# Gates that begin with x's rows, a feed-forward entered inside the attention, and scatters dealt over more rounds

## The reference

```python
x = x + L0_xattn(layernorm(x), ctx, ctx, gates)    # gates: tanh(cat(q,k,v) @ W + b), log_sigmoid, cumsum, running max
x = x + L0_ffn(layernorm(x), w1, b1, w2, b2)       # rmsnorm, rows rounded to 255 levels, weights to -1/0/1, gelu, the same again
x = x + L1_xattn(layernorm(x), ctx, ctx)           # phi = (elu + 1)**5, causal scores, normalised
x = x + L1_ffn(layernorm(x), gate, 8 experts)      # softmax over 8 experts, the best 2, gelu feed-forward of each
```

## Time and profile before

| | us |
|---|---|
| median of 3 runs | 611.01 (609.58 to 611.13) |
| the profiled execution: its time, its span | 610.62, 608.9 |
| busy: PE, DVE, ACT, POOL | 497.8, 399.3, 303.2, 352.3 |
| gates, first attention, feed-forward | 0 to 46.4, to 137.3, to 250.9 |
| second attention with routing, experts | to 365.7, to 608.9 |

### The profile page before, as it was taken

One profiled execution on the slowest core, in us unless ns is written; L12 is line 12 of the kernel. 1 busy time (PEld: TensorE's weight loads), 2 busy tenths in 40 slices (PEclk: granted clock), 3 DMA queues, 4 the chain that ended last, 5 costly groups with the idle time before them and its releaser, 6 DMA issues. The chain is left out here.

```text
span 608.9 us, 13847 instructions
## 1 busy us (share of the span) xinstructions
PE 497.8 (82%) x4467; PEld 365.9 (60%) x4467; DVE 399.3 (66%) x1228; ACT 303.2 (50%) x752; POOL 352.3 (58%) x421
## 2 busy tenths in 40 slices
PE   1979999997688878367666658999999999999960
PEld 1845776663355444246556526788878887888740
DVE  3432678998888888456988635566657676666540
ACT  0234575863789988567764313444344434443410
POOL 3509599782888878524686661445555555455531
PEclk9979999997999999857776678999999999999995
DMA  8733633320132232110142264233223323332225
GB/s 280 120 96 121 209 104 114 105 71 18 36 105 92 83 102 73 38 35 23 56 156 87 79 175 133 42 49 54 48 43 54 53 49 53 45 55 30 26 28 154
DMA packets 50614, 50.14 MB, mean 82 GB/s; under 512 B 21584, under 2 KB 40272, under 8 KB 50384
## 3 DMA queue, kind: packets, MB, share of 16 engines
q1 hardware_dynamic: 41168, 36.04, 20.2%
q0 software_dynamic: 7152, 9.36, 9.7%
q10 hardware_dynamic: 2224, 3.86, 2.0%
HBM read 36.46 MB, written 14.87 MB: 84 GB/s over the span
## 5 line engine op out<-in xcount | busy, mean ns | idle before, releaser
L1394 ACT ACTIVATE region<-cps,aux 128x128 f32<-128x128 f32 x312 | 89.3, 368 | 132.3 <-PE cps L1546 132.3
L1285 POOL CAST vaug<-region 128x512 bf16<-128x512 f32 x78 | 49.1, 630 | 107.9 <-ACT region L1394 96.2
L1546 PE MATMUL cps<-aux,w1hi 128*128 128x128 bf16 x1248 | 109.9, 219 | 0.9 <-DVE aux L1754 0.5
L1546 PE MATMUL cps<-aux,w1lo 128*128 128x128 bf16 x624 | 107.5, 217 | 0.0
L1559 PE MATMUL cps<-w2pair,vaug 128*128 x312 | 105.3, 379 | 0.0
L1546 PEld LDWEIGHTS cps<-aux,w1hi 128*128 x1248 | 95.9, 96 | 5.8 <-DVE aux L1754 0.7
L1562 PE MATMUL cps<-w2pair,vaug 128*128 x312 | 78.7, 273 | 0.0
L1291 POOL DMA_INDIRECT y_sum<-aux x39 | 61.0, 1564 | 15.7 <-issue 6.0
L1546 PEld LDWEIGHTS cps<-aux,w1lo 128*128 x624 | 61.5, 98 | 0.0
L1761 DVE TENSOR_TENSOR vaug<-region,vaug 128x512 bf16<-128x512 f32 x78 | 51.2, 697 | 0.1
L1769 DVE TENSOR_TENSOR aux<-cps,wstage 128x256 f32<-128x256 f32 x39 | 16.6, 425 | 52.7 <-PE cps L1559 51.7
(11 more groups left out here) (274 smaller groups left out, 1113.2 us busy)
## 6 DMA issues: line engine op xcount, KB each, us to landing
wstage<-in_wall SPq DMA_DIRECT2D x64, 256.0 KB, 2.6
aux<-row_buf SPq DMA_DIRECT2D x39, 129.5 KB, 2.1
x_all<-in_x SPq DMA_DIRECT2D x4, 512.0 KB, 8.9
w2pair<-in_ctxT ACTq DMA_DIRECT2D x2, 1024.0 KB, 11.5
vaug<-in_ctx SPq DMA_DIRECT2D x16, 128.0 KB, 4.0
aux<-in_ctxT SPq DMA_DIRECT2D x8, 256.0 KB, 3.0
y_sum<-x_all SPq DMA_DIRECT2D x8, 256.0 KB, 3.2
w2pair<-in_w1T SPq DMA_DIRECT2D x2, 512.0 KB, 4.7
```

The source lines that it names most:

```text
L1285: pool.tensor_copy(hhi[:, j % 3, n], hf[:, j % 2, n]).then_inc(hi_done, 1)
L1394: last = act.activation(hf[:, j % 2, f * BLK:(f + 1) * BLK], hp[:, j % 2, f, :], ACT.Gelu, bias=b1T[:, bass.ds(e * NF + f, 1)])
L1546: last = pe.matmul(hp[:, j % 2, f, :], w1(cc * NF + f, part), rowsT[:, j % 2, cc, xpart, :], start=(cc == 0 and n == 0), stop=(cc == NC - ...
```

## The change

1. Gates: TensorE transposes the first quarter of x's rows before the context's matmuls, which come in two halves, behind the first and the second quarter. VectorE takes the statistics of the first quarter before the gates' weights. The eight unused matmuls at the block's end go, and four open the attention's block.
2. Feed-forward: ScalarE centres tiles 0 and 1 within the attention's last rounds; VectorE scales tile 0 right behind the last `product`; the first rounding comes before the roots of sequence 6; the first table covers 8 tiles, not 4 (so the next `row_scales` and `tables` come later). `refined`, `scaled` and `residual` of the last sequence move into the tile loop, and so do the `row_stats` of sequence 5; those of 6 and 7 come two or three tiles later. 8 unused matmuls follow the first transposes in place of 16 ahead of them.
3. Routing: the scatters are dealt over the rounds by a table. Rounds 6 and 7 issue six in place of four each, and after the last `low_part` eight are left in place of twelve.
4. Ahead of the experts: 44 unused matmuls before the wait for the last scatters (28 before), and 5 behind it (10 before).

```diff
@@ gates, TensorE
-                    pe.wait_ge(zb_ready, 1)
-                    for half in range(2):
+                    def context_gates(half):
+                        if half == 0:
+                            pe.wait_ge(zb_ready, 1)
                         pe.wait_ge(kt_in[half], 16)
...
                         last.then_inc(tp_ready, 1)
+                        if q < 2:
+                            context_gates(q)
                         if q:
                             gates(q - 1)
...
-                    keep_running(8)
@@ gates, VectorE (gate_weights: the six operations that stood first)
-                        if q:
+                        if q == 0:
+                            gate_weights()
+                        else:
                             normalize(q - 1)
@@ attention and feed-forward, TensorE
+                    for _ in range(4):
+                        pe.matmul(unread, identb[:, :], flat(heads[:, 0:HG, :]), start=True, stop=True)
                     state(0)
...
-                    pe.wait_ge(pv1_read, B)
-                    keep_running(16)
                     first_transposes(0)
+                    pe.wait_ge(pv1_read, B)
+                    keep_running(8)
@@ ScalarE
-            SCALED_AT = (0, 4, 12, NT)
+            SCALED_AT = (0, 8, 12, NT)
...
+                        if n >= UN - 3 and n < UN - 1:
+                            centred(n - UN + 3)
-                    centred(0)
-                    centred(1)
-                    centred(2)
+                    first_rounded(0)
                     roots(B - 2)
                     squares(B - 1)
-                    first_rounded(0)
                     first_rounded(1)
+                    centred(2)
@@ GpSimd
-                    residual(B - 1)
...
-                        if i < 2:
-                            row_scales(i + 1)
+                        if i in (3, 5):
+                            row_scales((i - 1) // 2)
...
+                        if i == 0:
+                            residual(B - 1)
@@ VectorE
+                        if n == UN - 1:
+                            first_scale(0)
                     joined(B - 1)
-                    refined(B - 2)
-                    scaled(B - 2)
-                    denominators(B - 1)
-                    square_sums(B - 1)
-                    first_scale(0)
-                    row_stats(B - 3)
                     first_scale(1)
                     first_copied(0)
+                    denominators(B - 1)
+                    refined(B - 2)
+                    square_sums(B - 1)
                     first_copied(1)
-                    refined(B - 1)
-                    scaled(B - 1)
+                    scaled(B - 2)
...
-                        if j < 2:
-                            row_stats(B - 2 + j)
                         if j + 2 < NT:
                             first_scale(j + 2)
+                        if j == 1:
+                            refined(B - 1)
+                            scaled(B - 1)
+                        if 2 <= j <= 4:
+                            row_stats(B - 5 + j)
@@ routing, GpSimd
+            SCATTERED = {4: ((0,), (1,)), 5: ((2,), (3,)), 6: ((4,), (5, 6)), 7: ((7,), (8, 9)), 8: ((10,), (11,)), 9: ((12, 13), ())}
...
-                    for b in range(ENDS - 4, B):
-                        scatter(b, 0)
-                        scatter(b, 1)
+                    for i in range(NT - TB, NT):
+                        scatter(i)
@@ ahead of the experts, TensorE
-                    keep_running(28)
+                    keep_running(44)
                     pe.wait_ge(moved[(B - 1) % NPK], 16 * 2 * TB * (B // NPK))
-                    keep_running(10)
+                    keep_running(5)
```

More of the change, by code:

```diff
@@ L387, in _, with gate_weights @@
                     chain = Chain(dve, ch)
-                    dve.wait_ge(small_in, 48)
-                    dve.wait_ge(made, 1)
-                    for gate_, at in ((0, 56), (1, 120)):
-                        n = slice(gate_ * NH, gate_ * NH + NH)
-                        dve.tensor_copy(Z[:, 0:NC, at:at + NH], wif[:, 0:NC, n])
-                        dve.tensor_tensor(Z[:, NC:2 * NC, at:at + NH], wif[:, NC:2 * NC, n], wif[:, 2 * NC:3 * NC, n], ALU.add)
-                    dve.tensor_scalar(ifb, ifb, 1.0 / CAP, None, ALU.mult)
-                    dve.tensor_scalar(gain, gain, 1.0, None, ALU.add).then_inc(zb_ready, 1)
+                    def gate_weights():
+                        dve.wait_ge(small_in, 48)
+                        dve.wait_ge(made, 1)
+                        for gate_, at in ((0, 56), (1, 120)):
+                            n = slice(gate_ * NH, gate_ * NH + NH)
+                            dve.tensor_copy(Z[:, 0:NC, at:at + NH], wif[:, 0:NC, n])
+                            dve.tensor_tensor(Z[:, NC:2 * NC, at:at + NH], wif[:, NC:2 * NC, n], wif[:, 2 * NC:3 * NC, n], ALU.add)
+                        dve.tensor_scalar(ifb, ifb, 1.0 / CAP, None, ALU.mult)
+                        dve.tensor_scalar(gain, gain, 1.0, None, ALU.add).then_inc(zb_ready, 1)
                     def normalize(q):
@@ L732, in signs @@
                         act.wait_ge(weight_steps, 4 + q + 1)
-                        act.activation(dst, src, ACT.Sign, bias=magic[:, 1:2])
+                        act.activation(dst, src, ACT.Sign, bias=magic[:, 1:2]).then_inc(weight_steps, 1)
                     def centred(i):
                         act.wait_ge(vv_ready, i // TB + 1)
+                        if i == 0:
+                            act.wait_ge(weight_steps, 12)
                         if i >= NXC:
@@ L918, in refined @@
                         dve.wait_ge(rs_ready, b + 1)
+                        if b:
+                            dve.wait_ge(y_ready, b)
                         chain(dve.tensor_tensor(sc, rs, rs, ALU.mult))
@@ L1223, in low_part, with scatter @@
                         pool.tensor_tensor(packed_b[:, u, D:2 * D], xs[:, b % 2], packed_b[:, u, 0:D], ALU.subtract).then_inc(lo_ready, 1)
-                    def scatter(b, t):
+                    def scatter(i):
+                        b, t = i // TB, i % TB
                         g = group_of[b]
                         u = TB * (b % NPK) + t
-                        i = TB * b + t
                         if t == 0:
@@ L1261, in _ @@
                             roots((j + 1) // 2)
-                        s0 = 2 * (j - 4) if j >= 4 else None
-                        if s0 is not None:
-                            scatter(s0 // 2, 0)
+                        before, after = SCATTERED.get(j, ((), ()))
+                        for i in before:
+                            scatter(i)
                         if 1 <= j <= B:
                             squared_roots(j - 1)
-                        if s0 is not None:
-                            scatter(s0 // 2, 1)
+                        for i in after:
+                            scatter(i)
                         if j + 1 < B:
```

## The result

| | before | changed |
|---|---|---|
| median, same chip, 8 runs each | 610.38 us | 614.83 us |
| ratio | | 1.0073, 95% interval 1.0053 to 1.0093 |
| profiled execution: time, span | 610.62, 608.9 | 613.46, 611.7 |

The change makes the kernel 4.5 us slower (3.2 to 5.7). Forecast were 609.4, and 605.9 to 612.5.

A forecast was written before the change was run, and what follows sets the result against it. Stages follow each other: TensorE bounds gates and first attention, a GpSimd-VectorE ring the tile loop, GpSimd the routing's end. Terms 0.0 + 0.0 - 3.2 + 4.2 - 2.4 = -1.4 gave 609.4 us, range 605.9 to 612.5.

The forecast's parts named there:

- the sum of the tile loop: Feed-forward tile loop: added work costs 8.5 us against 4.3 before, +4.2; bounds +1.5 and +7.
- rival 3: Tile loop: VectorE operations in three row passes held up like L951, 1.20 instead of 0.2; with tables +2.9, 612.3; chance 0.06.
- four signs of being wrong: Loop 1 under 7.5 us; row passes not lengthening tiles 2-4; round 8's normed 4 us later; unused matmuls over 2 us past rows.
- Rival 1: Tile loop and entry: moved passes swallowed, clock perhaps up at the entry; -4.9, 605.9; chance 0.28.
- Into the feed-forward: Last product to first hidden: earlier scaling and rounding start hidden(0) at 147.0 instead of 150.17, -3.2; -5.2 at the upper clock.
- The attention's end: Attention's last rounds: ScalarE's two centred lie beside VectorE's work; without that cover they cost 1.0.
- Gates and opening: Gates net 0.0 (bounds -0.3, +0.3); attention's start taken as 0.0, from -1.4 to +1.5 by when the clock rises.
- Rival 4: Gates: first quarter's transposes do nothing for the clock's rise, which comes 1.7 later and costs 0.85; 610.2; chance 0.04.
- Routing: Routing's end: dealt-out scatters and the changed unused matmuls give -2.4, bounds -3.9 and +1.
- the -1.6 for the first load: Routing's end: last scatter issued 3.1 earlier, but zero fills start 2.0 later; the go comes at 364.1, -1.6.
- the -0.8 for fewer unused matmuls: Ahead of the experts: unused matmuls end at 367.4, before 370.15; routing taken as -2.4, the go alone -1.6.
- Rival 2: Routing: added scatters find no cover, four issues cost 5.1 instead of 2.0; +4.4, 613.8; chance 0.12.

The follow-up runs named there:

- the last residual back: Part 2, but refined, scaled and residual of the last sequence ahead of the tile loop as before, against the kernel before: 1.0045.
- the two entry kernels: Part 2's entry with the last sequence's steps and tables put back (1.0013), and that with centring and scaled of sequence 6 reordered (0.9948), against the kernel before.
- the entry alone: Part 2 with the last sequence's steps and tables put back and residual ahead of tile 0, against the kernel before: 1.0013.
- The order alone: Part 1's order of the gates, eight unused matmuls kept and none ahead of the attention, against the kernel before: 0.9970.
- the exchange of unused matmuls: The kernel before with the eight unused matmuls at the gates' end taken out and four ahead of the attention: 1.0014.
- part 2 put right: Changed kernel with last sequence's steps, tables, row passes put back, centring after the last exponential, scaled of sequence 6 early, against the kernel before: 0.9957.
- part 4 alone: The kernel before with 44 and 5 unused matmuls ahead of the experts in place of 28 and 10: 1.0004.

## Why the prediction was wrong

**The step that failed is the sum of the tile loop.** "Sum: ... = 8.5, against ... 4.3 before: +4.2." The changed trace has 12.1 over fifteen plain tiles of 5.68 (97.28 from `hidden(0)` to `hidden(15)`) against 4.2: +7.9, beyond the bound of +7. Tiles 0 and 1 were as worked out (-0.4 and +3.9, forecast -0.5 and +3.6), and so was tile 10. Tiles 2 to 6 were priced at 0.9, 0.9, 1.0, 0 and 1.3, in sum 4.1, and took 1.7, 1.2, 2.2, 0.8 and 1.9, in sum 7.8. (The 0.4 in the 4.3 is tile 3, 6.09 us before, for which I gave no row; and 44 unused matmuls come to 11.7 us by my prices, not 12.0. Neither matters.)

Most of the missing 3.7 us are rival 3's mechanism. I gave it 0.06 and priced one operation for each row pass; there are up to two in a pass (L959 and L960) and two in a table (L964, L965). Their excess over 0.15 to 0.22 in the rows above is 0.6, 1.5 and 1.8, with 0.4 for the third pass (at 170.18, not shown); 1.0 of it, L965, was in the price. That makes 3.3, as an estimate: it does not come out tile by tile, since tile 5 is 0.8 over with no such operation in it. The rest is the clock, for which I had no term: behind long tiles, in which TensorE waits, it stands at its lower level for a part of the next, and that tile is longer. Before, the clock was 0.74 in tile 2 and 1.00 in tiles 3 to 7; now it is 0.54 in tile 2 and 0.74 in tile 5. With the last residual back and tile 1 short again it is 1.00 in tiles 1 to 7, and tile 5, without extra work, takes 5.85 in place of 6.46; the pair of windows above (5.68 at 1.00, 6.45 at 0.74) is the same on one code.

That the held-up operations are GpSimd's doing is shown by the two entry kernels: the first and the third operation of `refined` took 1.27 and 1.12 beside the residual; where it began earlier, 0.87 (up to its end) and 0.17. And all 106 small operations of this kind (at most 16 numbers a row) that lasted over 0.35 us in the 16 traces, between 134 and 250 us, end 0.02 to 0.04 us behind an operation of GpSimd. The Trainium skill, "SBUF — State Buffer", "Who interferes with whom", has this as the shared port pair; these traces agree, by the 0.02 to 0.04 us between the ends. The trace of the kernel before had more of it than the one case that I priced, which should have raised rival 3:

```profile
140.44 1.25 DVE L908 SCALAR_TENSOR_TENSOR w2pair<-w2pair 128x16 f32<-128x16 f32 x1
```

None of the four signs of being wrong came: tile 1 took 9.55, the row passes did lengthen their tiles, `squared_roots` of round 8, which `normed` waits for, was 1.6 us later, not 4, and the unused matmuls ended before the rows. They looked for passes that cost nothing, not for passes that cost more than they last. Rival 1, passes swallowed, is out by the +7.9.

**Into the feed-forward** I said -3.2 and the trace says -4.0, but the reason was wrong, and the near number is luck. The early scaling and rounding gave nothing by themselves (13.9 with the entry alone). The gain came from taking the last sequence's `refined` and `scaled` out of the way, and tile 1 gave it back. The early entry is worth 2.3 us only when the residual of the sequence before runs early too.

**The attention's end** cost 0.8 that I held to be free, and at first I blamed the centring. With the centring hoisted and the table of 4 the attention took 85.85; with it hoisted and the table of 8, 86.7 in all four kernels that have both. GpSimd's `row_scales` lasts 1.65 in place of 1.02; with its weight pieces later by that, VectorE's `scaled` of sequence 5, the steps before it and a `w1lo` subtraction (at 127.03 and 128.85) meet differently:

```profile
128.89 1.66 DVE L941 TENSOR_TENSOR w2pair<-w2pair 128x512 f32<-128x512 f32 x1
```

It took 0.87 in the kernel before, at 131.15. That this longer one is the whole 0.8 is read, not tested by itself.

**Gates and opening**: forecast 0.0. The order alone gave -1.8 (-3.0 to -0.7), the exchange of unused matmuls +0.9 (-0.5 to +2.3), both together +1.0 (0 to +2.1). These do not add up within their middles, and the question stays open; a term near zero is not contradicted. Rival 4's delay of 1.7 us is not seen: in five traces with the new order the context matmuls began to follow each other at 0.22 us instead of 0.43 from 2.9 to 6.0 us after TensorE's first operation, in eleven with the old one from 3.1 to 5.6.

**Routing**: forecast -2.4. Part 3 gave -2.0 and part 4 +0.2. Part 3's time agrees with the -1.6 for the first load; the -0.8 for fewer unused matmuls was not there, since loads and the lower clock hold the second and third block. Rival 2 is out. One pair of traces said 0.0, and I believed it too quickly: from first `keys` to first load, the eleven kernels without the table have 107.6 to 112.7 us, 111.2 in the mean, the five with it 106.3 to 111.3, 109.0 in the mean. The way was not the one worked out: the last scatter, issued 3.4 us earlier in the changed kernel, landed late with the fills.

**The sum**: +1.0 +3.9 -2.0 +0.2 = +3.1 by the four parts, against 4.5 (3.2 to 5.7) together, on another chip. The terms for part 1, part 2 and parts 3 and 4 were 0.0, +1.0 and -2.4: 1.0, 2.9 and 0.6 too low. The largest is part 2's, and with part 2 put right the sign turns.

## What to carry to other kernels

Before work is moved into a ring's slack, list the small operations in it, and what the other engine does at that moment: an operation of 0.2 us took up to 1.2 here, and the slack of 0.5 was gone with the first. A move that takes a step off one wait wins only what the place it goes to does not charge; run the entry and the move apart. One trace of each kernel tells a microsecond's mechanism but not its average: the same gates and opening ended up to 3 us apart in three traces.

## What the runs showed of the hardware

TensorE's pace in the gates differs between executions of one code: the 32 context matmuls took 8.68 to 9.87 us, since they began to follow each other at 0.22 us instead of 0.43 from 3.1 to 5.6 us after the first. It looks like the rise of the clock, but the profile's granted clock says 1.00 there all the time.

Which small VectorE operations GpSimd holds up can be counted. In the 16 traces, between 134 and 250 us, 75 `tensor_scalar` on 2 to 8 numbers a row and two-input operations on 16 began well within an operation of GpSimd (0.35 us or more ahead of its end). 57 of them lasted until its end, up to 1.27 us; the other 18, of 0.16 and 0.17 us, all stood beside `row_scales`. The 453 `tensor_scalar` on one number and the 164 reciprocals that began so were not held up.

At the last rank of the routing TensorE's increment of its semaphore was recorded 0.18 us after the matmul's start in the changed kernel, and 6.3 us after it in the kernel with part 4 alone, where VectorE idled 7.14 us. Nine of the eleven traces without the scatters' table show an idle time of 7.1 us there, and none of the five with it: three have 3.0. The kernel before, the changed one and two more have 1.0, so the pair at the head of this document does not show it. Where VectorE waits so long, the table takes part of the wait away, which may be where its gain lies. What holds the increment is not known.
